# VectorE instead of ScalarE copies an attention unit's sums out of PSUM

## The reference

```
scores = q @ k.T * scale            # per head: 2048 x 2048
scores = where(causal, scores, -big)  # second and third attention
probs = softmax(scores)
out = probs @ v                     # per head: 2048 x 8
```

## Time and profile before

| | us |
|---|---|
| median of 3 runs | 2534.18 (2530.25 to 2537.48) |
| the profiled execution, its own time | 2535.02 |
| its span | 2533.3 |
| PE busy in the span | 2193.3 (87%) |
| DVE busy | 1763.0 (70%) |
| ACT busy | 1529.7 (60%) |
| POOL busy | 363.6 (14%) |

### The profile page before, as it was taken

The page is one execution under the profiler, slowest core; times in us unless marked ns, Lnnn a source line. Parts: engine busy times, 40 slices in busy tenths (PEclk is TensorE's granted clock), DMA queues, the critical chain, the costliest instruction groups (busy, mean ns, idle before and its releaser), DMA issues. The chain is left out here.

```text
span 2533.3 us, 41305 instructions
## 1 busy us (share of the span) xinstructions
PE 2193.3 (87%) x14544; PEld 998.6 (39%) x14544; DVE 1763.0 (70%) x3989; ACT 1529.7 (60%) x2361; POOL 363.6 (14%) x562
## 2 busy tenths in 40 slices
PE   4799999999995389999977995799999778979797
PEld 2434434444332143333433442433334334734473
DVE  4788888888843588887844554788878476438544
ACT  1188888888892038887751221388877544934592
POOL 2100100111000100011120001000111234304330
PEclk7599999999997659999997997599999888989898
DMA  4510200000000251010100002510101034604550
GB/s 149 115 31 9 32 12 8 13 7 13 3 5 2 108 80 27 13 29 18 32 13 0 0 0 101 87 27 13 30 18 30 15 124 160 208 9 150 165 185 17
DMA packets 79654, 130.30 MB, mean 51 GB/s; under 512 B 16688, under 2 KB 38960, under 8 KB 78128
## 3 DMA queue, kind: packets, MB, share of 16 engines
q1 hardware_dynamic: 76160, 117.63, 17.9%
q10 hardware_dynamic: 3312, 10.33, 1.4%
HBM read 53.13 MB, written 15.20 MB: 27 GB/s over the span
## 5 line engine op out<-in xcount | busy, mean ns | idle before, releaser
L868 ACT ACTIVATE att_probs<-psum 128x1024 f32<-128x1024 f32 (+3 forms) x1152 | 1036.1, 957 | 213.4 <-PE psum L927 210.9
L810 DVE TENSOR_REDUCE att_part_max<-psum 128x1 f32<-128x512 f32 x1280 | 816.9, 683 | 109.2 <-PE psum L909 106.9
L909 PE MATMUL psum<-k_rows,att_q_rows 64*128 64x512 f32 (+3 forms) x2304 | 712.5, 487 | 30.7 <-DMA k_rows<-k_pieces 10.8
L909 PEld LDWEIGHTS psum<-k_rows,att_q_rows 64*128 64x128 f32 x2304 | 341.4, 196 | 567.5 <-DVE att_part_max L810 239.6
L927 PE MATMUL psum<-att_q_rows,k_rows 64*128 64x512 f32 (+3 forms) x2304 | 456.1, 408 | 29.4 <-ACT att_probs L868 12.5
L952 PE MATMUL psum<-att_probs,v_aug 128*9 128x512 f32 (+3 forms) x3712 | 426.6, 532 | 3.7 <-POOL att_probs L732 2.3
L927 PEld LDWEIGHTS psum<-att_q_rows,k_rows 64*128 64x128 f32 x2304 | 239.7, 187 | 158.9 <-ACT att_probs L868 139.5
L854 ACT ACTIVATE att_rise<-psum 128x512 f32<-128x512 f32 x256 | 153.2, 600 | 241.3 <-PE psum L909 206.1
L807 DVE CUSTOM_DVE_ANT_0 att_masked<-psum,mask_max_sb 128x128 bf16<-128x128 f32 (+3 forms) x512 | 233.6, 484 | 35.7 <-PE psum L909 32.5
L796 DVE CUSTOM_DVE_ANT_0 att_rise<-psum,att_rise 128x512 f32<-128x512 f32 x256 | 175.2, 691 | 73.2 <-PE psum L909 48.2
L732 POOL TENSOR_SCALAR_AFFINE_SELECT att_probs<-att_probs 128x256 f32<-128x256 f32 x256 | 103.0, 408 | 731.1 <-ACT att_probs L868 728.4
(11 more groups left out here) (257 smaller groups left out, 2154.6 us busy)
## 6 DMA issues: line engine op xcount, KB each, us to landing
lproj_swapped<-lproj_other SPq DMA_DIRECT2D x128, 128.0 KB, 2.1
latt_k<-local_k_T SPq DMA_DIRECT2D x32, 384.0 KB, 3.0
k_rows<-k_pieces SPq DMA_DIRECT2D x36, 320.0 KB, 11.2
att_q_rows<-q_pieces SPq DMA_DIRECT2D x168, 64.0 KB
lproj_table<-in_tables SPq DMA_DIRECT2D x16, 512.0 KB, 4.2
latt_q<-local_q_T SPq DMA_DIRECT2D x32, 256.0 KB, 2.4
latt_v_seen<-local_v_tok SPq DMA_DIRECT2D x64, 128.0 KB, 2.4
latt_v_seen<-local_v_tok SPq DMA_DIRECT2D x32, 256.0 KB, 2.3
```

The source lines that it names most:

```text
L810: nc.vector.tensor_reduce(column, ring[e][:, 0:w], AX.X, ALU.max).then_inc(ring_free, 1)
L868: nc.scalar.activation(probs[s % NPROBS][:, pr, :, at:BANK], st[pr][:, :, at:BANK], ACT.Exp, scale=scale).then_inc(st_free, 1)
L909: nc.tensor.matmul(ring[e][:, 0:w], q_rows[u % NQ][rows, pr, qt * P:(qt + 1) * P].bitcast(F32R), k_rows[b][rows, pr, keys + kc * BANK:keys ...
```

## The change

The copy goes from ACT to DVE. On DVE it is done in the loop over the maxima tiles, ahead of the first tile that PE issues after the first step of the next unit, with the same two waits and the same signal. Where the list of tiles is at its end, the copies that are left come behind it.

```diff
@@ vector
+            def take_z(u):
+                dve.wait_ge(pv_done, plan.first_step[u + 1])
+                if u >= 2:
+                    dve.wait_ge(z_out[u % 2], ZOUT * (u // 2))
+                nc.vector.tensor_copy(z_sb[u % 2][:, :], z_ps[:, :]).then_inc(z_free, 1)
+
+            z_taken = 0
             for e, (u, *tile) in enumerate(stream):
+                while z_taken < NU - 1 and e == plan.after[plan.first_step[z_taken + 1]]:
+                    take_z(z_taken)
+                    z_taken += 1
                 if e == plan.begun_at[u]:
                     dve.wait_ge(parts_set, u + 1)
...
+            for u in range(z_taken, NU):
+                take_z(u)
@@ scalar
-            def take_z(u):
-                act.wait_ge(pv_done, plan.first_step[u + 1])
-                if u >= 2:
-                    act.wait_ge(z_out[u % 2], ZOUT * (u // 2))
-                nc.scalar.activation(z_sb[u % 2][:, :], z_ps[:, :], ACT.Copy).then_inc(z_free, 1)
...
                 if s >= NPROBS:
                     act.wait_ge(pv_done, s - NPROBS + 1)
-                if u > 0 and kb == 1:
-                    take_z(u - 1)
...
-            take_z(NU - 1)
```

## The result

| | before | after |
|---|---|---|
| median, us | 2533.5 | 2564.8 |
| ratio to before | | 1.0131, interval 1.0108 to 1.0154 |
| the profiled execution, its own time | 2535.0 | 2564.8 |
| its span | 2533.3 | 2563.1 |
| first attention, first to last exponential | 640.7 | 657.4 |

The kernel is slower by 1.3%, about 31 to 33 us; 2565 us were forecast. (Median and ratio of after are those of three runs, 2561 to 2574 us; a fourth took 3354 us at a granted clock of 0.553 throughout, and with it the median is 2569.2.) "All else" is the span less the three attentions. Over the executions of this case it lies between 1144 and 1162 us whichever kernel ran, so its -3.4 us is not the change's.

The account below looks back on a forecast made before the run. PE was taken as the bound, ACT running behind it. Terms 19.9 + 5.3 + 4.5 + 2.8 - 1.5 + 0.3 = 31.3 us on 2534.2 gave 2565 us; own range 2557 to 2574 (64%), 8 in 10: 2547 to 2577.

Parts of the forecast that it names:

- The place of the copy: At each boundary, DVE reaches the copy behind queued maxima tiles, later than PE needs it in 30 of 45.
- 14 boundaries of the first attention: Copy goes in front of the fifth of five maxima; PE's products start 1.42 us late, 19.9 us in all.
- the four first causal ones: First two boundaries of each causal attention: PE's products start 1.33 us late, 5.3 us in all.
- six (0.75): Boundaries 4 to 6 of both causal attentions: PE's products start 0.75 us late, 4.5 us in all.
- six (0.46): Boundaries 8 to 10 of both causal attentions: PE's products start 0.46 us late, 2.8 us in all.
- the signs: What would show the forecast right, among them ACT's busy time down 29 us and PE's product loads waiting 30 to 40.
- Does the lateness stay?: Whether PE's late starts persist after each boundary: bounded at +17 to +49 us in all, neither taken.
- The rival that had PE with room: Absorbed: at late boundaries 0.46 us or more of each stall is given back; 2551 us, between 2543 and 2557; 18%.
- The delay in the trace of before: Second attention's products start 0.33 us late against the third's at one boundary; the unit took 0.34 us longer.
- the load share of 40%: In the first attention, PE's weight loads are busy for 254.9 of 640.7 us.
- The other 15 boundaries: Causal boundaries 3, 7, 11 to 15 and the first attention's 15th: -1.5 us together, ends +1 and -6.
- Faster, with ACT as the bound: Rival: ACT sets the pace, so boundaries gain the 9.0 us that PE waits for ACT's copy; 2525 us; 5%.

Follow-up runs that it names:

- where it was tried: Extra DVE instruction at each boundary: at the copy's place in the kernel before, 2533.7 us; behind the copy in the changed kernel, 2568.1 us.
- with the waits filled: Changed kernel with four matmuls, result overwritten unread, given to PE during its wait for DVE's copy at ten causal boundaries: 2563.9 us, ratio 1.0133.
- with 1.90 us: Changed kernel with an extra DVE instruction ahead of each copy, PE's wait growing from 1.29 to 1.90 us: 2619.7 us, ratio 1.0309.

## Why the prediction was right

**The mechanism.** PE waits for DVE's copy at the boundaries where DVE gets there late. The place of the copy was the argument, and moving it by two tiles takes the whole loss away; DVE's time alone costs next to nothing (2.4 to 2.5 us where it was tried).

**The terms.** How late PE's products start against before, counted from the unit's first exponential: 1.36 us at 14 boundaries of the first attention (1.42 forecast); 1.28 at three of the four first causal ones (1.33) and 0.95 at the fourth, which was 0.33 late before; 0.71 at six (0.75); 0.42 at six (0.46). The copy takes 0.685 us in place of 0.692 and PE follows it after 0.05 us, not 0.1. PE waits 29.0 us in all by its matmuls and 43.5 by its loads, where 30 to 40 were forecast. ACT's busy time fell by 21 us and not by the 29 named among the signs, which are 48 times the 0.60 of a copy and not the 0.48 by which one sets ACT back.

**Does the lateness stay?** Nearly. The pattern behind takes back 0.09 us of it, and the 14 late units of the first attention grow by 1.17 to 1.41 us each (the second from 40.47 to 41.69), 17.5 us together where 19.9 were forecast; its first and last unit got 0.8 us shorter, so that it grew by 16.7. The rival that had PE with room falls: it wanted 0.46 us back at each. The delay in the trace of before told the truth, and the load share of 40% was no sign of room: PE took back under a tenth of the wait. The Trainium skill, Perfetto Trace Analysis, section Identifying the Most-Contended Engine, says to judge TensorE's headroom by MFU (its floating-point work as a share of the peak) and by the load share; by the load share alone this kernel would have had room, and it had next to none.

**The mis-sized terms.** The causal attentions were forecast at 5 to 6 us each. Their waits alone are worth about 4: with the waits filled they grew by 374.1 - 370.0 = 4.1 and 375.5 - 370.2 = 5.3 us, 9.4 together, of which about 1.3 are the filler's own 0.2 us at six boundaries; and the 16.5 us measured for both less some 8 for the half clock leave 8.5. The half clock was not in the sum at all: the rows of before showed 0.98 to 0.99 (the 0.98 holds its one stretch of 3.4 us in the last unit), and no boundary where a matmul waits for the copy to learn from. So that the sum of 31 us came out to within 2 us was luck: the waits were put some 5 us too high in all (19.9 against 17, 11 against 8 to 9), and a term of some 8 us was missing. The mechanism and the range don't hang on that luck: the waits as measured, without the half clock, would be about 2560 us, still in the forecast's own range.

**The other 15 boundaries.** A gain of 1.5 us was taken. About that is there, by the lengths of the units and not by PE's start. The units that begin at boundaries 3 are 0.2 us longer, as their products start 0.2 late (0.3 were read); those that begin at boundaries 7 take 25.8 us in place of 26.1; and the last unit of each attention, in which ACT's exponentials no longer wait behind a copy, is 0.4 us shorter (in the third, apart from the half clock that before has there). At boundaries 11 to 15 the products start when they did.

**The rivals.** Faster, with ACT as the bound: the 9.0 us of waits for ACT's copy bought nothing even where DVE's copy came early enough, since they were waits of PE's loads beside a busy PE. That rival's price, and the occupancy of 86 against 82% that spoke for it, were both beside the point.

## What to carry to other kernels

When a copy that frees a buffer moves to another engine, its price is not the duration on the new engine but the moment at which that engine's queue reaches it, against the moment at which the buffer is needed: the same copy cost 31 us behind two tiles and nothing ahead of them. Look up both moments in the timeline for each kind of boundary before choosing the place in the queue. A wait that stands in the rows of the weight loads alone, with no idle matmul beside it, need not be on the path: here 9.0 us of such waits were worth nothing. And count a wait that opens on a busy TensorE twice where the trace has no such wait yet: its own time, and the half clock that may follow it.

## What was not expected of the hardware

A wait of 1.2 us on PE was followed by the half clock at some boundaries and not at others of the same kind in the same execution (1.21 and 1.22 us above). Even waits of 0.64 us were: two of the six in the changed kernel, at 1846.7 and 1877.5 us. In the first attention a wait of 1.29 us at 14 boundaries never was followed by it, in any of five profiles that have it; with 1.90 us, nine of 14 were. Why the first attention bears the shorter wait and the causal ones often don't was not tried. The steps ahead of a causal boundary are the narrow ones of the diagonal, in which PE does a little less: in the changed kernel it was busy for 9.3 of the 10 us ahead of the third attention's first wait, and for 9.9 of those ahead of the first attention's.
